# Moving the four loads of W_out to another DMA queue, and one sum of signs to a later place on VectorE

## The chip, the cores and the metric

The kernel runs on one core of a Trainium2 chip, in one launch. The metric is the time of the execution on the device in microseconds, as the median of repeated runs. Lower is better. A profile of one execution stands beside it; its span runs from the first to the last instruction of the core.

## The reference

Two layers read the same normalised input and are added to it: a linear attention with decay over chunks of 128 tokens, and a feed-forward network with ternary weights that keeps the 204 largest of 2048 hidden values of each token. Cut to what matters:

```python
# attention layer: B=4, T=1024, E=512, 16 heads of 32, chunks of 128
q, k, v = (x @ Wq), (x @ Wk), (x @ Wv)          # per head
q, k = _rotary(q), _rotary(k)
def step(kv, qkv):
    qi, ki, vi = qkv
    inter = jnp.einsum('bhcd,bhde->bhce', qi * q_decay[None, :, :, None], kv)
    scores = jnp.einsum('bhcd,bhsd->bhcs', qi, ki) * dmask[None]
    intra = jnp.einsum('bhcs,bhse->bhce', scores, vi)
    kv_new = r_C[None, :, None, None] * kv + jnp.einsum('bhcd,bhce->bhde', ki * k_decay[None, :, :, None], vi)
    return (kv_new, inter + intra)
attn = _rms_norm(attn, rms_w); return attn @ Wo
# feed-forward layer: N=2048
def ternary_quant(W):
    scale = jnp.mean(jnp.abs(W))
    q = jnp.clip(jnp.round(W / (scale + 1e-08)), -1.0, 1.0) * scale
    return W + jax.lax.stop_gradient(q - W)
z = x_flat @ ternary_quant(W_syn).T + b_syn
topv, _ = jax.lax.top_k(z, k)                    # k = 204 of 2048
hidden = jnp.where(z >= topv[:, -1:], jax.nn.relu(z), 0.0)
out = hidden @ ternary_quant(W_out).T + b_out
return layernorm(x + out, gamma, beta)
# both together
xn = _layernorm(x)
return x + attention(xn) + feed_forward(xn)
```

The mean of |W| over the whole matrix fixes the threshold of its ternary form, so no sign of W_out can be taken before all of W_out was read and summed.

## The kernel before

The 4096 tokens are 32 tiles of 128. A prologue prepares the weights, and then 31 steps run as a pipeline: in the step of tile t, TensorE makes the projections of tile t+1, the attention of tile t, the attention's output product of tile t-1 and the feed-forward's second product (`network_high`, `network_low`) of tile t-2. Each engine has its own program in its own `@block`, written out by hand; instructions of an engine run in that order, and semaphores (`wait_ge`, `then_inc`) hold them to one another. DMAs that SyncE issues go through its queue, those that ScalarE issues through another one. Before the change ScalarE issues the loads of Wq, Wk, Wv and of the four quarters of W_syn, and SyncE everything else, all transpositions by DMA among it.

W_out comes in four quarters of 1 MB, `out_in[0]` to `out_in[3]` (128 partitions with 8 KB each). Their places are used by others before. Quarters 2 and 3 lie where quarters 0 and 1 of W_syn were (the tile `woutT`), so they wait until these were made ternary (`syn_tern` 1, `syn_sign` 2). Quarter 0 lies in `hl`, where the ternary quarter 0 of W_syn is read by a DMA transposition (`synT0`) and, as its neighbour, by TensorE (`syn_flip`). Quarter 1 lies in a part of `area1` that nothing uses earlier. ScalarE then takes the sum of absolute values of each quarter (`sums("out", ...)`, L374) into a column of `pc`; its full-size output goes to `signs_b`, a scratch area (half of `pair_b`) that Wo's absolute sum (`wo_rows`, L398) and others also use, so that they run in one fixed order. TensorE sums the columns over the partitions (`sums_spread`, L877), and from the mean come the thresholds.

In the prologue VectorE makes the first guess of tile 0's threshold from the statistics of z (L1355, `guess_ready`). In the step of tile 0 ScalarE counts with that guess (`first_count`, L524), refines twice, and VectorE writes the masked copy of z (`below`, L1522), from which it takes maxima of 16 segments (`segments`, L1423). In between it makes the high and low halves of Wo (L1361, L1366).

The signs of W_out are taken by ScalarE (`sign("out", ...)`, L380), two for each quarter, and added by VectorE (`ternary_of_signs`, L1373 and L1377). SyncE transposes each quarter into `woutT` (`out_transpose`, L300). Quarter 1's ternary form lies in `hT`'s place, so the transposition of tile 0's hidden values (`high_transposed`, L308) waits for `outT1`, and TensorE's first `network_high` (L1043) waits for that and for all four quarters. `following_step` is VectorE's order in the step of tile 1.

## Time and profile before

| what | value |
|---|---|
| median of 3 runs | 987.05 us (986.56 to 988.97) |
| the profiled execution | 988.97 us, its span 987.2 us |
| TensorE (PE) busy | 931.5 us, 94% of the span |
| VectorE (DVE) busy | 861.2 us, 87% |
| GpSimd (POOL) busy | 757.8 us, 77% |
| ScalarE (ACT) busy | 591.2 us, 60% |
| mean granted clock of TensorE | 0.980 |

Busy time is an average over the whole; in the first 120 us, where the weights are prepared, the shares are lower and the engines wait for each other in turn. The timelines of the engines there, with the idle time in front of an instruction and what ended it, tell which wait comes last. The DMA share is that of 16 engines which all queues use together. The granted clock is 1.00 at 2.4 GHz and 0.50 at 1.2 GHz.

### The profile page before, as it was taken

What the parts mean: (1) busy time and instruction counts of PE and PEld (TensorE: products, weight loads), DVE (VectorE), ACT (ScalarE), POOL (GpSimd) and SP (SyncE); (2) the same over time, 40 slices, a digit from 0 to 9 for tenths busy, and PEclk for the clock granted to TensorE, in tenths of its full rate; (3) what the DMA queues carried; (4) which work ended last, traced back from release to release, by engine and by line L of the source; (5) the groups of instructions that cost most, each with busy time, mean ns of one, the idle gap of its engine ahead of it and who ended that gap; (6) DMA issues with size and microseconds to landing.
All of it is one profiled execution on the core that took longest, in us unless ns stands there. A gap on an engine that the chain in (4) does not pass through costs nothing.

```text
span 987.2 us, 19245 instructions
## 1 busy us (share of the span) xinstructions
PE 931.5 (94%) x6771; PEld 485.9 (49%) x6771; DVE 861.2 (87%) x2289; ACT 591.2 (60%) x782; POOL 757.8 (77%) x655
## 2 busy tenths in 40 slices
PE   5838799999999999999999999999999999999977
PEld 2414355554555555545555555455555554555533
DVE  6869688988889889889898898888988988989886
ACT  6778466665556666655566666555666665556551
POOL 1655768889888888898888888988888889888653
PEclk9977899999999999999999999999999999999999
DMA  9856645465555555565446546654466466444550
GB/s 326 266 174 115 118 78 115 89 119 118 97 93 83 115 103 101 119 117 92 92 86 118 113 92 118 117 98 89 85 118 110 94 118 115 98 92 83 97 97 32
DMA packets 322372, 111.08 MB, mean 113 GB/s; under 512 B 308449, under 2 KB 308705, under 8 KB 321505
## 3 DMA queue, kind: packets, MB, share of 16 engines
q1 hardware_dynamic: 318432, 102.42, 53.0%
q10 hardware_dynamic: 3840, 7.41, 2.1%
q8 instruction: 54, 0.88, 0.4%
q14 instruction: 46, 0.37, 0.1%
HBM read 24.34 MB, written 8.39 MB: 33 GB/s over the span
## 4 chain that ended last, share of the span: by engine, by line
PE 86%; DVE 5%; DMA 3%; issue 2%; ACT 1%; POOL 1%; SPq 1%; ACTq 0%; DVEq 0%; POOLq 0%
PE proj L933 44%; PE p_ffn L1043 11%; PE p_ffn L1051 10%; PE p_wo L1065 8%; PE p_av L1005 3%; PE sbank L996 3%; PE p_av L1016 3%; PE sbank L941 1%; DMA area<-hl 1%; DMA hl<-in_L_ffn_W_out_dram 1%; PE sbank L1108 1%; DMA area<-in_L_attn_Wq_dram 1%; SPq L269 0%; DMA woutT<-area 0%; SPq L264 0%
## 5 line engine op out<-in xcount | busy, mean ns | idle before, releaser
L933 PE MATMUL proj<-wqkv,xT 128*128 128x512 f16 x1152 | 261.5, 385 | 0.0
L933 PE MATMUL proj<-wsynT,xT 128*128 128x512 f16 x1024 | 238.9, 382 | 0.0
L933 PEld LDWEIGHTS proj<-wqkv,xT 128*128 128x128 f16 x1152 | 112.5, 99 | 127.8 <-issue 5.9
L933 PEld LDWEIGHTS proj<-wsynT,xT 128*128 128x128 f16 x1024 | 95.0, 98 | 100.9 <-issue 1.7
L743 POOL TENSOR_TENSOR hl<-area,hl 128x2048 f16<-128x2048 f32 x31 | 127.6, 4116 | 5.4 <-ACT hl L543 5.4
L1043 PE MATMUL p_ffn<-woutT,area 128*128 128x512 f16 x496 | 122.0, 391 | 7.9 <-DMA area<-hl 7.9
L1051 PE MATMUL p_ffn<-woutT,area 128*128 128x512 f16 x496 | 112.3, 379 | 0.0
L458 ACT ACTIVATE area<-area 128x1024 f16<-128x1024 f32 x64 | 64.1, 1049 | 77.4 <-POOL area L697 77.4
L1423 DVE MAX8 cand<-area 128x8 f32<-128x128 f32 x512 | 107.7, 277 | 1.1
L1311 DVE SCALAR_TENSOR_TENSOR area<-proj,c,gb 128x512 f32<-128x512 f32 x128 | 92.6, 744 | 5.3 <-PE proj L933 2.8
L748 POOL TENSOR_TENSOR ahl<-pair_a,ahl 128x512 f16<-128x512 f32 x32 | 37.1, 1159 | 78.0 <-DVE area L1522 75.2
L1522 DVE SCALAR_TENSOR_TENSOR area<-area,c 128x2048 f32<-128x2048 f32 x32 | 93.3, 2917 | 1.1
L1065 PE MATMUL p_wo<-wo,ahl 128*128 128x512 f16 x384 | 88.6, 380 | 2.4 <-POOL ahl L748 2.4
L548 ACT ACTIVATE pair_b<-pair_b,c 128x512 f32<-128x512 f32 x31 | 25.2, 812 | 103.4 <-DVE c L1517 103.4
L1475 DVE SCALAR_TENSOR_TENSOR area<-area,c 128x2048 f32<-128x2048 f32 x31 | 84.0, 2709 | 0.0
L517 ACT ACTIVATE diag<-ident,c 128x128 bf16<-128x128 f32 x32 | 12.9, 402 | 114.9 <-DVE c L1404 114.9
L1051 PEld LDWEIGHTS p_ffn<-woutT,area 128*128 128x128 f16 x496 | 48.5, 98 | 58.3
L1043 PEld LDWEIGHTS p_ffn<-woutT,area 128*128 128x128 f16 x496 | 47.2, 105 | 56.1 <-DMA area<-hl 8.3
L702 POOL TENSOR_TENSOR area<-area 128x512 f16<-128x512 f32 x64 | 74.7, 1190 | 0.0
L793 POOL TENSOR_TENSOR kvs<-state,rc 128x128 f32<-128x128 f32 x31 | 69.9, 2255 | 0.0
L543 ACT ACTIVATE hl<-area 128x2048 f16<-128x2048 f32 x31 | 59.2, 1909 | 16.5 <-DVE area L1475 16.5
L529 ACT ACTIVATE Pr<-area,c 128x2048 f16<-128x2048 f32 x32 | 63.8, 1993 | 0.9 <-DVE c L1482 0.9
(237 smaller groups left out, 1817.5 us busy)
## 6 DMA issues: line engine op xcount, KB each, us to landing
xrn<-in_L_attn_x_dram SPq DMA_DIRECT2D x32, 256.0 KB, 3.0
out_dram<-pair_b SPq DMA_DIRECT2D x32, 256.0 KB, 2.0
woutT<-in_L_ffn_W_syn_dram ACTq DMA_DIRECT2D x2, 1024.0 KB, 10.7
area<-in_L_ffn_W_syn_dram ACTq DMA_DIRECT2D x2, 1024.0 KB, 11.9
woutT<-in_L_ffn_W_out_dram SPq DMA_DIRECT2D x2, 1024.0 KB, 6.5
area<-in_L_attn_Wq_dram ACTq DMA_DIRECT2D x1, 1024.0 KB, 7.0
area<-in_L_attn_Wk_dram ACTq DMA_DIRECT2D x1, 1024.0 KB, 9.3
area<-in_L_attn_Wv_dram ACTq DMA_DIRECT2D x1, 1024.0 KB, 11.5
```

The costliest lines, as they stand in the source:

```text
L458: nc.scalar.activation(qks[:, m, :, 0:2 + m:1 + m, :], src.unsqueeze(2).to_broadcast([P, H, 2, DH]), ACT.Copy).then_inc(S["qk_hi"], 1)
L702: nc.gpsimd.tensor_tensor(qks[:, m, :, 2 - m, :], qk[:, b.par, m * E:(m + 1) * E].rearrange("p (h d) -> p h d", h=H), qks[:, m, :, 0, :], ...
L743: nc.gpsimd.tensor_tensor(hl[:, 1, :], src, hl[:, 0, :], ALU.subtract).then_inc(S["lo_ready"], 1)
L793: nc.gpsimd.tensor_tensor(kvs.rearrange("p (g e) -> p g e", g=HG), state.rearrange("p (g e) -> p g e", g=HG), k.unsqueeze(2).to_broadcast( ...
L933: last = nc.tensor.matmul(bank, xT[:, b.par, k, :], w, start=m == 0, stop=m == len(pairs) - 1)
L1043: nc.tensor.matmul(p_ffn, hT[:, k, :], woutT[:, k, :], start=k == 0, stop=False)
L1051: last = nc.tensor.matmul(p_ffn, hT[:, NB + k, :], woutT[:, k, :], start=False, stop=k == NB - 1)
L1065: last = nc.tensor.matmul(p_wo, ahl[:, l, g, :], wo[:, w, g, :], start=m == 0, stop=m == len(terms) - 1)
L1311: nc.vector.scalar_tensor_tensor(z[:, b.par, n * 512:(n + 1) * 512], proj[(b.par + 3 + n) % 2], gs, gb[:, n * 512:(n + 1) * 512], ALU.mult ...
L1423: nc.vector.max(cand[:, 0, 8 * n:8 * n + 8], masked[:, n * SEG:(n + 1) * SEG]).then_inc(S["seg_done"], 1)
L1475: nc.vector.scalar_tensor_tensor(dst, z[:, u.par, :], thr, z[:, u.par, :], ALU.is_ge, ALU.mult).then_inc(S["h_ready"], 1)
L1522: nc.vector.scalar_tensor_tensor(masked, z[:, t.par, :], t2, z[:, t.par, :], ALU.is_le, ALU.mult).then_inc(S["w_out"], 1)
```

## The change

The loads of W_out move from SyncE's queue to ScalarE's. Quarter 1 is issued in the prologue right after the last quarter of W_syn. Quarters 2 and 3 are issued after ScalarE's two signs of W_syn's quarter 1; ScalarE waits there for `syn_tern` 1. Quarter 0 is issued after tile 1's third projection was evicted, behind waits for `synT0` and `syn_flip` 4. The sum of quarter 1 is taken right behind that, ahead of the evictions of the flipped signs (`syn_flat`), and Wo's sum comes after it; the other three sums keep their place. On VectorE, in the step of tile 1, the sum of signs of quarter 1 moves from a place ahead of the second chunk of z (`z_chunk(b, 1)`) to one behind it, behind the addition of the attention, the last maxima and `so`, which itself moves ahead of the selection.

```diff
--- before.py
+++ after.py
@@ -237,9 +237,6 @@
             def load_x(n):
                 load(xr[:, n % RING, :], x[n * P:(n + 1) * P, :], f"x_loaded{n % 2}")
 
-            def load_out(q):
-                load(out_in[q], W_out.rearrange("(b p) n -> p b n", p=P)[:, q, :], f"out_loaded{q}")
-
             def load_tables():
                 load(gb, rows(b_syn, N), "rows_loaded")
                 for dst, src in ((qdec, t_qdec), (kdec, t_kdec), (rc, t_rc), (keep, t_keep), (iota, t_iota)):
@@ -280,18 +277,11 @@
                 load_wo()
                 load_x(2)
                 syn_transposed(0, 1)
-                load_out(2)
-                sp.wait_ge(S["syn_sign"], 2)
-                load_out(3)
                 load(boutx, rows(b_out, E), "bb_loaded")
                 load(bet, rows(beta, E), "bb_loaded")
                 load(gam, rows(gamma, E), "bb_loaded")
                 syn_transposed(2, 2)
                 qk_transposed(Tile(0, 0))
-                load_out(1)
-                sp.wait_ge(S["synT0"], 16)
-                sp.wait_ge(S["syn_flip"], 4)
-                load_out(0)
                 load(dmask, t_dmask, "dmask_loaded")
 
             def out_transpose(q):
@@ -367,8 +357,10 @@
                     act.wait_ge(S[f"{w}_loaded{q}"], 16)
 
                     n = 4 * (w == "out") + q
-                    if w == "out":
-                        act.wait_ge(*(S["wo_abs"], 1) if q == 2 else (S["out_abs"], (3, 1, 0).index(q) + 1))
+                    if w == "out" and q == 1:
+                        act.wait_ge(S["syn_flip"], 4)
+                    elif w == "out":
+                        act.wait_ge(*(S["wo_abs"], 1) if q == 2 else (S["out_abs"], 2 if q == 3 else 3))
                     else:
                         act.wait_ge(*(S["qkv_abs"], 3) if q == 0 else (S["syn_abs"], 1))
                     nc.scalar.activation(signs_b, (out_in if w == "out" else syn_in)[q], ACT.Abs,
@@ -394,7 +386,7 @@
             def wo_rows():
 
                 act.wait_ge(S["wo_scaled"], KB)
-                act.wait_ge(S["syn_flip"], 4)
+                act.wait_ge(S["out_abs"], 1)
                 nc.scalar.activation(signs_b, wo_in.rearrange("p b n -> p (b n)"), ACT.Abs,
                                      accum_out=pc[:, 57:58]).then_inc(S["wo_abs"], 1)
 
@@ -420,6 +412,9 @@
             def load_syn(q):
                 act.dma_start(syn_in[q].rearrange("p (b d) -> p b d", d=E),
                               W_syn.rearrange("(b p) d -> p b d", p=P)[:, 4 * q:4 * q + 4, :]).then_inc(S[f"syn_loaded{q}"], 16)
+
+            def load_out(q):
+                act.dma_start(out_in[q], W_out.rearrange("(b p) n -> p b n", p=P)[:, q, :]).then_inc(S[f"out_loaded{q}"], 16)
 
             def out_mean():
                 act.wait_ge(S["out_sum"], 1)
@@ -486,6 +481,7 @@
                 qkv_sums(1)
                 load_syn(2)
                 load_syn(3)
+                load_out(1)
                 qkv_sums(2)
                 normalised(second)
                 qkv_high(1)
@@ -500,15 +496,23 @@
 
                 sign("syn", syn_in[1], syn_other[1], syn_thr[1])
                 sign("syn", syn_in[1], syn_t[1], syn_thr[0])
+                act.wait_ge(S["syn_tern"], 1)
+                load_out(2)
+                act.wait_ge(S["syn_sign"], 2)
+                load_out(3)
                 qkv_out(second, 1)
                 qk_high(first)
                 sign("syn", syn_in[3], syn_other[3], syn_thr[1])
                 sign("syn", syn_in[3], syn_t[3], syn_thr[0])
                 qkv_out(second, 2)
+                act.wait_ge(S["synT0"], 16)
+                act.wait_ge(S["syn_flip"], 4)
+                load_out(0)
+                sums("out", (1,))
                 syn_flat(3)
                 heads_state(first)
                 wo_rows()
-                sums("out", (2, 3, 1, 0))
+                sums("out", (2, 3, 0))
 
             def diagonal(u):
 
@@ -1597,14 +1601,14 @@
                 z_chunk(b, 0)
                 probs(t, 2)
                 probs(t, 3)
-                ternary_of_signs(1, 9)
                 z_chunk(b, 1)
                 attention_added(u)
                 segments(t, 3)
-                selection(t)
                 dve.wait_ge(S["out_mean"], 1)
                 then(nc.vector.scalar_tensor_tensor(so, scale_out, 0.5 * XS / 16384.0, pc[:, 43:44], ALU.mult,
                                                     ALU.mult))
+                ternary_of_signs(1, 9)
+                selection(t)
                 z_chunk(b, 2)
 
             def step(dve, i, p):
```

The number of instructions of TensorE, VectorE and GpSimd, and their kinds, stay as they are; TensorE's and GpSimd's order too. Below, a row is a line of the kernel, the operation with output and inputs, and the semaphores that it waits for. First ScalarE in the prologue, around the signs of W_syn's quarter 1 (the sign into `hl`) before:

```order
L436 ACTIVATE area<-proj 128x512 [waits qkv_done]
L380 ACTIVATE pair_b<-woutT,pc 128x2048 [waits syn_thr]
L380 ACTIVATE hl<-woutT,pc 128x2048 [waits syn_thr]
L436 ACTIVATE area<-proj 128x512 [waits qkv_done]
L458 ACTIVATE area<-area 128x16x64 [waits rot_step]
```

and after:

```order
L431 ACTIVATE area<-proj 128x512 [waits qkv_done]
L372 ACTIVATE pair_b<-woutT,pc 128x2048 [waits syn_thr]
L372 ACTIVATE hl<-woutT,pc 128x2048 [waits syn_thr]
L417 DMA woutT<-in_L_ffn_W_out_dram 128x2048 [waits syn_tern]
L417 DMA woutT<-in_L_ffn_W_out_dram 128x2048 [waits syn_sign]
L431 ACTIVATE area<-proj 128x512 [waits qkv_done]
L453 ACTIVATE area<-area 128x16x64 [waits rot_step]
```

Two loads of W_out now stand between the signs and the next eviction of a projection, each with its wait. Further on ScalarE evicts, sums and counts. Before, from the eviction of tile 1's v to the last sum:

```order
L436 ACTIVATE v<-proj 128x512 [waits qkv_done]
L475 ACTIVATE wsynT<-sbank 128x512 [waits syn_flip] x2
L475 ACTIVATE wsynT<-p_av 128x512 [waits syn_flip]
L475 ACTIVATE wsynT<-p_ffn 128x512 [waits syn_flip]
L468 ACTIVATE stateD<-state 32x4x32 [waits constants]
L468 ACTIVATE stateD<-state 32x4x32 x3
L398 ACTIVATE pair_b,pc<-area 128x2048 [waits syn_flip,wo_scaled]
L374 ACTIVATE pair_b,pc<-woutT 128x2048 [waits wo_abs,out_loaded2]
L374 ACTIVATE pair_b,pc<-woutT 128x2048 [waits out_abs,out_loaded3]
L374 ACTIVATE pair_b,pc<-area 128x2048 [waits out_abs,out_loaded1]
L374 ACTIVATE pair_b,pc<-hl 128x2048 [waits out_abs,out_loaded0]
```

and after, from the same eviction on:

```order
L431 ACTIVATE v<-proj 128x512 [waits qkv_done]
L417 DMA hl<-in_L_ffn_W_out_dram 128x2048 [waits syn_flip,synT0]
L366 ACTIVATE pair_b,pc<-area 128x2048 [waits syn_flip,out_loaded1]
L470 ACTIVATE wsynT<-sbank 128x512 [waits syn_flip] x2
L470 ACTIVATE wsynT<-p_av 128x512 [waits syn_flip]
L470 ACTIVATE wsynT<-p_ffn 128x512 [waits syn_flip]
L463 ACTIVATE stateD<-state 32x4x32 [waits constants]
L463 ACTIVATE stateD<-state 32x4x32 x3
L390 ACTIVATE pair_b,pc<-area 128x2048 [waits out_abs,wo_scaled]
L366 ACTIVATE pair_b,pc<-woutT 128x2048 [waits wo_abs,out_loaded2]
L366 ACTIVATE pair_b,pc<-woutT 128x2048 [waits out_abs,out_loaded3]
L366 ACTIVATE pair_b,pc<-hl 128x2048 [waits out_abs,out_loaded0]
```

The load into `hl` and the sum of quarter 1 (`area`, `out_loaded1`) have come in front of the evictions into `wsynT`. On SyncE's queue nothing takes the place of the four loads: the bias rows follow the transposition of W_syn's quarter 0, and the load of `dmask` follows the two of tile 0's q and k.

On VectorE, in the step of tile 1, the weighting of the scores (L1388), the sum of signs (into `area`), the chunk of z, the attention's addition and the maxima stood like this:

```order
L1388 SCALAR_TENSOR_TENSOR pair_a<-sbank,c,dmask 128x512 [waits ss_done,al_ready,scores_done] x2
L1373 TENSOR_TENSOR area<-area,pair_b 128x2048 [waits out_sign]
L1311 SCALAR_TENSOR_TENSOR area<-proj,c,gb 128x512 [waits z_done]
L1397 SCALAR_TENSOR_TENSOR xrn<-p_wo,c,xrn 128x512 [waits factor_step,beta_added,wo_done]
L1423 MAX cand<-area 128x8 [waits top_step,w_out]
L1423 MAX cand<-area 128x8 x3
L1528 TENSOR_SCALAR c<-c 128x1 [waits sum3]
```

and now:

```order
L1392 SCALAR_TENSOR_TENSOR pair_a<-sbank,c,dmask 128x512 [waits ss_done,al_ready,scores_done] x2
L1315 SCALAR_TENSOR_TENSOR area<-proj,c,gb 128x512 [waits z_done]
L1401 SCALAR_TENSOR_TENSOR xrn<-p_wo,c,xrn 128x512 [waits factor_step,beta_added,wo_done]
L1427 MAX cand<-area 128x8 [waits top_step,w_out]
L1427 MAX cand<-area 128x8 x3
L1608 SCALAR_TENSOR_TENSOR c<-c,pc 128x1 [waits out_mean]
L1377 TENSOR_TENSOR area<-area,pair_b 128x2048 [waits out_sign,seed]
L1532 TENSOR_SCALAR c<-c 128x1 [waits sum3]
```

The sum of signs has gone behind the four others.

## Rows read from the trace of the kernel before

**Rows 1.** The page, part 4: the chain that ended last, by engine

```profile
PE 86%; DVE 5%; DMA 3%; issue 2%; ACT 1%; POOL 1%; SPq 1%; ACTq 0%; DVEq 0%; POOLq 0%
```

**Rows 2.** Waits of TensorE (PE), 135 to 980 us: total, times, longest

```profile
PE p_ffn L1043 <- DMA area<-hl: 2.8, 1, 2.8
```

**Rows 3.** Timeline of TensorE: start, us, engine, line, op, [idle before <-releaser]

```profile
50.42 0.27 PE L860 MATMUL p_ffn<-ident,pc 128*1 128x128 f32 x1 [0.54 <-ACT pair_b L398]
...
74.81 0.61 PE L996 MATMUL sbank<-area 96*128 96x128 f16 x4 [9.57 <-DVE Pr L1388]
...
105.88 1.89 PE L933 MATMUL proj<-wsynT,xT 128*128 128x512 f16 x8
...
117.89 3.60 PE L1043 MATMUL p_ffn<-woutT,area 128*128 128x512 f16 x8 [5.14 <-DMA area<-hl]
```

**Rows 4.** Timeline of ScalarE (ACT) from 25 to 65 us

```profile
34.96 0.57 ACT L436 ACTIVATE area<-proj 128x512 f32<-128x512 f32 x1
...
41.31 0.60 ACT L436 ACTIVATE v<-proj 128x512 f32<-128x512 f32 x1
44.67 1.20 ACT L475 ACTIVATE wsynT<-sbank 128x512 f16<-128x512 f32 x2 [2.77 <-PE sbank L888]
...
62.60 1.91 ACT L374 ACTIVATE pair_b<-hl 128x2048 f16<-128x2048 f32 x1 [1.64 <-DMA hl<-in_L_ffn_W_out_dram]
...
64.51 1.99 ACT L524 ACTIVATE Pr<-area,c 128x2048 f16<-128x2048 f32 x1
```

**Rows 5.** Timeline of VectorE (DVE) from 58 to 71 us

```profile
58.00 0.43 DVE L1355 SCALAR_TENSOR_TENSOR c<-pc 128x1 f32<-128x1 f32 x1
...
66.94 2.34 DVE L1366 SCALAR_TENSOR_TENSOR wo<-area,pc,wo 128x2048 f16<-128x2048 f32 x1
...
70.01 2.35 DVE L1522 SCALAR_TENSOR_TENSOR area<-area,c 128x2048 f32<-128x2048 f32 x1
```

**Rows 6.** Timeline of GpSimd (POOL) at 59 us

```profile
59.52 1.65 POOL L663 TENSOR_TENSOR c<-c 128x1 f32<-128x1 f32 x1 [0.74 <-DVE c L1301]
```

**Rows 7.** Timeline of SyncE's queue (SPq) from 35 to 40 us

```profile
35.42 1.95 SPq L269 DMA_TRANSPOSE wsynT<-hl  x1
37.42 1.57 SPq L235 DMA_DIRECT2D woutT<-in_L_ffn_W_out_dram  x2
```

**Rows 8.** DMA issues, 37 to 40 us: last number is us to landing

```profile
wsynT<-hl SPq DMA_TRANSPOSE x1, 4.4
```

**Rows 9.** Windows: stretch, us, busy us of each engine, PEclk, DMA share, GB/s

```profile
15.00:20.00 5.00, 4.63 (x14) 1.71 (x12) 3.16 (x15) 4.01 (x6) 1.18 (x1) 1.00 1.05 386
20.00:25.00 5.00, 5.00 (x25) 2.62 (x24) 4.90 (x6) 5.00 (x5) 0.45 (x1) 1.00 0.74 275
80.00:85.00 5.00, 4.71 (x66) 2.73 (x58) 4.76 (x20) 4.42 (x6) 3.86 (x5) 0.92 0.81 149
120.00:125.00 5.00, 5.00 (x22) 1.99 (x21) 2.24 (x10) 1.11 (x2) 1.92 (x3) 0.83 1.14 207
```

**Rows 10.** DMA queues, 6 to 7 us: packets, MB, share; q10 is ScalarE's

```profile
q10 hardware_dynamic: 174, 0.35, 93.6%
q1 hardware_dynamic: 132, 0.02, 12.9%
```

**Rows 11.** Timeline of VectorE from 108 to 115 us

```profile
108.44 0.74 DVE L1311 SCALAR_TENSOR_TENSOR area<-proj,c,gb 128x512 f32<-128x512 f32 x1
...
109.76 0.85 DVE L1423 MAX8 cand<-area 128x8 f32<-128x128 f32 x4
...
114.14 0.83 DVE L1606 SCALAR_TENSOR_TENSOR c<-c,pc 128x1 f32<-128x1 f32 x1
```

**Rows 12.** The chain in order of time: start us, us, what

```profile
106.84 1.69 DVE area L1373
108.54 4.84 DMA woutT<-area
113.45 4.40 DMA area<-hl
```

## Prediction, made before the changed kernel was run

> **What bounds the kernel now.** I read the page first: TensorE makes up 86% of the chain that ended last, over a span of 987.2 us [rows 1]. From 135 us on TensorE waits almost nowhere, 2.8 us at its worst place [rows 2]. So the body runs at TensorE's pace, and nothing in it is touched. What the change can move is the moment at which TensorE enters that body: its row at 117.89 us, the first product with W_out's transpose, after 5.14 us idle for a DMA [rows 3]. A microsecond there is a microsecond of the whole, since later waits are too few to absorb it.
>
> Then I read the timelines of the start. The engines are late twice. First, ScalarE finishes the last absolute sum of W_out only at 64.4 us, because that quarter lands at 62.6, and its next instruction, the first count of tile 0, starts at 64.51 [rows 4]. VectorE had the guess that this count wants at 58.43 (58.00 and 0.43) [rows 5]. TensorE's 9.57 us idle before 74.81 is the same delay passed on through VectorE [rows 3]. Second, before 117.89 the chain is VectorE's sum of signs of quarter 1 (106.75 to 108.44), its transposition issued at 108.54, and the transposition of tile 0's hidden values, which waits for that one [rows 11, 12].
>
> **Part one: the loads of W_out move to ScalarE's queue.** Quarter 1 is issued 40 us earlier, behind W_syn. At 386 GB/s a quarter takes 2.7 us [rows 9], so it lands long before 42 us. The issue costs ScalarE at most 0.8 us of its queue (two in 1.57 us on SyncE's) [rows 7], beside work with about as much slack: nothing.
>
> Quarters 2 and 3 now make ScalarE wait for `syn_tern` 1, which comes when SyncE's transposition goes, at 35.42 [rows 7]. ScalarE was ready at 34.96 [rows 4], so 0.46 us of wait and two issues of 0.4 to 0.8 us: 1.2 to 2.0, I take 1.4 us. Behind them stand one eviction of a projection, the cast of tile 0's q and k, the signs of W_syn's quarter 3 and another eviction. That last one starts at 41.31 now and would start at 42.7 and end at 43.3. ScalarE is idle for 2.77 us after it, before 44.67 [rows 4]; this idle time covers the 1.4 us, as long as it isn't used twice.
>
> It is used twice, by quarter 0. ScalarE now waits for `synT0` before it may issue that load, and the sum of quarter 1 comes next, 1.91 and 0.1 us as the sum at 62.60 [rows 4]. The transposition behind `synT0` lands 4.4 us after its issue at 35.42, at 39.8 [rows 8]. But that was with quarters 2 and 3 behind it in its own queue; now they run beside it. No row shows a load beside a transposition. From below: an even split of the engines' time adds as much as the transposition itself needs, some 2.7 us, so 42.5, and ScalarE doesn't wait. From above: both loads are served first, 5.4 us, so 45.2. The nearest row is between 6 and 7 us, where both queues have work: 174 packets of one against 132 of the other, though the first moved 0.35 MB and the second 0.02 [rows 10]. Turns go by packet there, not by bytes, and W_out's rows are 8 KB where the transposition's packets are small, so I take 45.2. ScalarE then issues at 45.2, sums to 47.7, and its evictions of the flipped signs start at 47.7 instead of 44.67, 3.0 us later. So does the absolute sum of Wo (L398), for which TensorE's row at 50.42 waits [rows 3]. Behind that row stand the third and fourth chunk of tile 0's z, and with them the guess: 58.43 becomes 61.4. With the even split it is 43.3 plus 0.5 for the issue plus 2.0, 45.8 instead of 44.67: 1.1 us, and the guess at 59.6.
>
> The three remaining sums, 2.1 us apart each, follow the Wo sum and end about 59.6, before that guess. So the count starts with the guess. From there the path to VectorE's masked copy (70.01) takes: GpSimd's power op, which ends 2.74 us after the guess (59.52 and 1.65) [rows 6]; 0.2 us for the row shift; the low half of Wo, 2.3 (66.94 now); and 0.8 to the copy, as now from 69.2 to 70.01 [rows 5]. That is 6.1 us instead of 11.6. The gain is 5.5 us less what the guess loses: **5.5 − 3.0 = 2.5 us**, or 5.5 − 1.1 = 4.4 with the even split. Down to 106 us I find VectorE, ScalarE and GpSimd handing each other work without a fixed date in between, so all of it moves along. The masks that were loaded behind quarter 0 leave earlier: no cost.
>
> **Part two: VectorE's sum of signs of quarter 1 goes behind four other things.** Now it runs when `probs` ends, at 106.75. In its new place the third chunk of z comes first; it waits for TensorE's product at 105.88, which takes 1.89 us [rows 3], so it starts at 107.8. It and attention's addition take 1.3 us (108.44 to 109.76 now), the four maxima 0.8, and `so` between nothing and the 0.83 that it has at 114.14; I take 0.2 to 0.3, as its neighbours on one column mostly overlap [rows 11]. The sum starts at about 110.1 and, at the 1.69 us it takes now, ends at 111.8 instead of 108.44. The bounds are 3.1 and 4.0 by `so` alone. **The cost is 3.4 us**: the transposition that leaves at 108.54 leaves that much later, and nothing else was last there. What moves ahead gains nothing, since TensorE had its third chunk in time. Selection is later by the same sum, and its flag is wanted only in the middle of the product at 117.89 [rows 3].
>
> **The clock.** TensorE's idle time before 117.89 grows from 5.1 to some 8.5 us. After the 5.1 us the granted clock stays at the 1.2 GHz level until about 121.7 (a mean of 0.83 from 120 to 125), 3.8 us; after the 9.57 us before 74.81, until about 80.8 (0.92 from 80 to 85), 5.6 us from the restart at about 75.2 [rows 3, 9]. Half of 1.8 us is at most 0.9; by the length of the gap I take 0.3.
>
> **The sum**: −2.5 + 3.4 + 0.3 = +1.2 us, for a span of 988.4. The profiled execution took 988.97 us, 1.8 more than its span, and the median is 987.05; against the median, which is what will be compared, that is **988.2 us**. A measurement of this kernel tells 0.3%, 3.0 us, from no change.
>
> **Rivals.** (1) *Even split*: −4.4 + 3.4 + 0.3 = −0.7, 986.3 us. For it: the packets of a transposition might be grouped. Against: the counts [rows 10].
>
> (2) *Loads and transpositions slow each other down*. Place: DMA engines from 36 us on, where W_syn's two transpositions, quarters 2, 3 and 0 and the bias rows come to some 15 us of work in two queues. If the mixture runs a fifth slower, `synT0` and W_syn's second transposition land 2 to 3 us later, TensorE and ScalarE wait for them, and the gain of 2.5 is gone: +3.4 + 0.3, and up to 1 more. Time 991. It decides against the kernel from a loss of 1.8 us there (990.0). For it: quarter 0 will stand in front of W_syn's second transposition. Against: where both queues have loads, they move 0.37 MB in a microsecond together, close to one queue's 386 GB/s [rows 9, 10].
>
> (3) *No byte lands sooner*. Then ScalarE still waits for W_out as now, the first gain is 0, and the time is 987.05 + 3.7 = 990.8. Against it: from 20 to 25 us the DMA engines are busy for only 0.74 of the time [rows 9], which is room for quarter 1, and quarter 0 no longer stands behind it.
>
> The Trainium skill speaks against the change here: "DMA: Bandwidth & Descriptors", in its rules for kernel authors, says that spreading DMAs over several issuing engines gives no bandwidth and saves only issue time. Taken alone it gives rival 3; no row here contradicts it on bandwidth, and what the change has besides is the earlier date of issue.
>
> (4) *The second part is free*: some other wait is last before 117.89. Then −2.5 or −4.4 stands alone, some 983.5 us. Against it: the chain has the two transpositions back to back, 108.54 and 4.84 us, then 113.45 and 4.40 [rows 12].
>
> **Chances.** Forecast 0.50, rival 1 0.25, rival 2 0.13, rival 3 0.04, rival 4 0.08. The range: below, the even split with 3.1 and no clock loss, 985.7, and a little for the spread of the runs; above, 4.0 and 0.9 on the forecast give 989.5, and it reaches into rival 2: 985.3 to 990.7. Faster by over 0.3% (under 984.1) is most of rival 4 alone: 0.07. Slower (over 990.0) is rivals 2 and 3, less the milder half of each's range: 0.15. Within: 0.78.
>
> **What would show it.** `synT0`'s landing at 45.2 against 42.5; ScalarE's sum of quarter 1 around 46; the first count at 61.5 (59.7 with rival 1); the masked copy at 67.5; the transposition of quarter 1 issued at about 109.4; TensorE's first W_out product at 118.8, or 117 and less with rival 1. TensorE entering before 115 or after 121 would make the prediction wrong, and so would any new wait of TensorE behind 135 us.

## The result, and the profile after

The changed kernel takes 992.7 us (median of 6 runs, 990.6 to 996.4) against 987.2 us for the kernel before beside it (6 runs, 985.9 to 989.0): a ratio of 1.0058, 95% interval 1.0035 to 1.0082. Measured again on another occasion (the run e3_after_again below) the ratio was 1.0042, 1.0027 to 1.0056. The change makes the kernel 4 to 5.5 us slower. The prediction said 988.2 us, 1.2 us slower and within what can be told from no change; it was wrong, and 992.7 lies above its range. (One execution of the kernel before, out of 84, took 1401.9 us; medians are hardly touched by it.)

The profiled execution of the changed kernel took 989.12 us, with a span of 987.1, so the two profiled executions are equally long. The one of before, 988.97 us, stands high among its runs, and the one of after lies below all six timed runs of its kernel. Where they part again is told at the end of this section. First the chain that ended last by engine, from the page, for [rows 1]:

```profile
PE 85%; DMA 4%; DVE 4%; POOL 3%; issue 3%; SPq 0%; ACT 0%; ACTq 0%; DVEq 0%; POOLq 0%
```

and TensorE's wait from 135 to 980 us, for [rows 2]:

```profile
PE p_ffn L1047 <- DMA area<-hl: 1.6, 1, 1.6
```

The body still runs at TensorE's pace. TensorE's timeline, for [rows 3], with two more rows of the same stretch (start us, us, engine, line, operation, idle time ahead and its releaser):

```profile
46.96 3.61 PE L937 MATMUL proj<-wsynT,xT 128*128 128x512 f16 x16 [2.98 <-DMA wsynT<-hl]
54.56 0.27 PE L864 MATMUL p_ffn<-ident,pc 128*1 128x128 f32 x1 [3.98 <-ACT pair_b L390]
54.92 3.18 PE L937 MATMUL proj<-wsynT,xT 128*128 128x512 f16 x8
...
74.98 0.61 PE L1000 MATMUL sbank<-area 96*128 96x128 f16 x4 [11.03 <-DVE Pr L1392]
...
120.70 3.32 PE L1047 MATMUL p_ffn<-woutT,area 128*128 128x512 f16 x8 [7.87 <-DMA area<-hl]
```

TensorE enters the body at 120.70 instead of 117.89 us, 2.81 later. It is idle for 2.98 us for the first transposition of W_syn, which it did not wait for before, and for 3.98 us where it waited 0.54 us. ScalarE, for [rows 4]:

```profile
46.85 0.33 ACTq L417 DMA_DIRECT2D hl<-in_L_ffn_W_out_dram  x1
47.28 1.91 ACT L366 ACTIVATE pair_b<-area 128x2048 f16<-128x2048 f32 x1 [5.29 <-DMA wsynT<-hl]
...
49.19 1.06 ACT L470 ACTIVATE wsynT<-sbank 128x512 f16<-128x512 f32 x2
...
52.41 1.91 ACT L390 ACTIVATE pair_b<-area 128x2048 f16<-128x2048 f32 x1
...
58.69 1.91 ACT L366 ACTIVATE pair_b<-hl 128x2048 f16<-128x2048 f32 x1
...
64.23 2.00 ACT L528 ACTIVATE Pr<-area,c 128x2048 f16<-128x2048 f32 x1 [3.54 <-DVE c L1359]
```

The last sum of W_out starts at 58.69 us instead of 62.60, 3.9 us sooner, as the change wants it. But the first count starts at 64.23, only 0.28 us sooner than before, because it now waits 3.54 us for VectorE's guess. VectorE, for [rows 5] and [rows 11]:

```profile
63.77 0.43 DVE L1359 SCALAR_TENSOR_TENSOR c<-pc 128x1 f32<-128x1 f32 x1
...
70.17 2.35 DVE L1526 SCALAR_TENSOR_TENSOR area<-area,c 128x2048 f32<-128x2048 f32 x1
...
109.22 0.86 DVE L1427 MAX8 cand<-area 128x8 f32<-128x128 f32 x4
110.00 0.14 DVE L1608 SCALAR_TENSOR_TENSOR c<-c,pc 128x1 f32<-128x1 f32 x1
110.17 1.73 DVE L1377 TENSOR_TENSOR area<-area,pair_b 128x2048 f16<-128x2048 f16 x1
```

The guess has moved from 58.00 to 63.77, by 5.8 us, and the masked copy from 70.01 to 70.17: the whole gain of the earlier loads is gone at that point. The sum of signs then starts at 110.17 instead of 106.75. The chain in order of time, for [rows 12]:

```profile
110.17 1.74 DVE area L1377
111.91 0.02 issue
111.93 4.25 DMA woutT<-area
...
116.24 4.41 DMA area<-hl
```

SyncE's queue and the landings, for [rows 7] and [rows 8] (the number at the end of the second piece is us from issue to landing):

```profile
34.33 5.80 SPq L266 DMA_TRANSPOSE wsynT<-hl  x1
```

```profile
wsynT<-hl SPq DMA_TRANSPOSE x1, 12.5
```

The same transposition that landed 4.4 us after its issue now takes 12.5 us, and its issue holds SyncE for 5.80 us instead of 1.95. What the queues moved shows why. For [rows 10], first the microsecond from 38 to 39 before the change, when the transposition was alone:

```profile
q1 hardware_dynamic: 836, 0.21, 116.7%
```

then the one from 40 to 41 in the changed kernel, where ScalarE's queue (q10) has quarters 2 and 3:

```profile
q10 hardware_dynamic: 40, 0.33, 78.0%
q1 hardware_dynamic: 46, 0.01, 5.2%
```

Forty packets of 8 KB and 46 of 256 bytes: in this microsecond the queues take turns packet by packet, so the transposition gets 46 packets through in the time in which it had 836. From 36 to 38 us it gets none through at all.

**The end of the two profiled executions.** TensorE reaches the scores of the last tile at 951.45 us, against 948.98 before, so 2.5 of the 2.8 us are still there. The last step gives them back. TensorE's first `network_high` of the last step, before the change:

```profile
958.84 3.59 PE L1043 MATMUL p_ffn<-woutT,area 128*128 128x512 f16 x8 [2.77 <-DMA area<-hl]
```

and after it:

```profile
960.59 1.90 PE L1047 MATMUL p_ffn<-woutT,area 128*128 128x512 f16 x8 [1.59 <-DMA area<-hl]
```

Eight products take 3.59 us in one execution, at the 1.2 GHz level, and 1.90 us in the other, at 2.4 GHz. The changed kernel is 1.75 us late at the start of this row and level at its end. That differs from one execution to the next (in a second profiled one of the changed kernel the same row took 2.72 us), and is why the medians, and not this pair, carry the comparison.

### The profile page after: what moved, and what is told of

The parts are those of the page before. It is cut to its first block, busy times and chain, and to the rows that moved or that the text cites. A ratio compares the mean times of both kernels' runs of the same rounds, so it can differ in the third digit from the quotient of the medians.

```text
span 987.1 us, 19245 instructions
## 1 busy us (share of the span) xinstructions
PE 929.5 (94%) x6771; PEld 484.8 (49%) x6771; DVE 858.9 (87%) x2289; ACT 590.8 (60%) x782; POOL 758.8 (77%) x655
## 4 chain that ended last, share of the span: by engine, by line
PE 85%; DMA 4%; DVE 4%; POOL 3%; issue 3%; SPq 0%; ACT 0%; ACTq 0%; DVEq 0%; POOLq 0%
PE proj L937 44%; PE p_ffn L1047 11%; PE p_ffn L1055 10%; PE p_wo L1069 8%; PE p_av L1009 3%; PE p_av L1020 3%; PE sbank L1000 3%; PE sbank L945 1%; DMA area<-in_L_ffn_W_syn_dram 1%; DMA area<-in_L_attn_Wk_dram 1%; PE sbank L1112 1%; DVE cand L1427 1%; DMA area<-in_L_attn_Wo_dram 1%; DMA area<-area 0%; DMA area<-hl 0%
## 5 line engine op out<-in xcount | busy, mean ns | idle before, releaser
L1047 PE MATMUL p_ffn<-woutT,area 128*128 128x512 f16 x496 | 118.8, 383 | 9.5 <-DMA area<-hl 9.5
L1055 PE MATMUL p_ffn<-woutT,area 128*128 128x512 f16 x496 | 112.3, 379 | 0.1
L706 POOL TENSOR_TENSOR area<-area 128x512 f16<-128x512 f32 x64 | 72.7, 1157 | 0.0
```

The costliest lines, as they stand in the source:

```text
L706: nc.gpsimd.tensor_tensor(qks[:, m, :, 2 - m, :], qk[:, b.par, m * E:(m + 1) * E].rearrange("p (h d) -> p h d", h=H), qks[:, m, :, 0, :], ...
L1047: nc.tensor.matmul(p_ffn, hT[:, k, :], woutT[:, k, :], start=k == 0, stop=False)
L1055: last = nc.tensor.matmul(p_ffn, hT[:, NB + k, :], woutT[:, k, :], start=False, stop=k == NB - 1)
```

## The experiments

Two theories stand against each other for the 4 to 5.5 us. A: the order on VectorE costs 3.4 us as predicted, and the loads fail to bring their 2.5 us, because they collide with the transpositions of W_syn (rival 2 of the prediction). B: the loads bring what was predicted and the order on VectorE, or the two together, costs more. All kernels of one batch ran beside the kernel before: 987.16 us in the first (e1 to e5), 987.45 in the second (e6 to e9), 987.62 in the third (e10 to e13).

| kernel | first product with W_out's transpose, us | median us (lowest to highest, runs) | ratio to before |
|---|---|---|---|
| before | 117.89 | 987.16; 987.45; 987.62 | 1 |
| e1 loads only | 117.71 | 988.42 (985.5 to 995.4, 12) | 1.0019 [1.0000, 1.0038] |
| e2 order on VectorE only | 120.58 | 990.43 (988.9 to 991.5, 8) | 1.0030 [1.0018, 1.0042] |
| e3 the change again | 121.00 | 991.20 (988.3 to 996.0, 12) | 1.0042 [1.0027, 1.0056] |
| e5 quarter 1 only | 114.33 | 983.23 (982.8 to 984.4, 5) | 0.9960 [0.9946, 0.9973] |
| e6 = e5, quarter 0 earlier | 113.40 | 983.26 (981.7 to 984.5, 5) | 0.9956 [0.9943, 0.9969] |
| e7 quarters 1, 0 on ScalarE | 116.21 | 986.88 (985.6 to 988.1, 11) | 0.9995 [0.9986, 1.0004] |
| e8 quarters 1, 2, 3 on ScalarE | 114.64 | 985.66 (982.2 to 992.5, 12) | 0.9987 [0.9969, 1.0006] |
| e9 = e6, bias rows later | 117.42 | 986.77 (984.7 to 987.2, 11) | 0.9987 [0.9979, 0.9996] |
| e10 = e5 + order on VectorE | 117.70 | 987.96 (986.2 to 988.8, 10) | 1.0004 [0.9994, 1.0013] |
| e11 = e5, quarters 2, 3 after `synT0` | 118.39 | 988.10 (986.2 to 989.4, 12) | 1.0001 [0.9991, 1.0012] |

The second column is from each kernel's one profiled execution. Median less first product is 868.9 to 871.0 us in every row, while the first product moves by 7.6 us: the moment at which TensorE enters the body sets most of the time, as the prediction had it. It sets the time to 2 or 3 us and not better: taken from one and the same execution, the time less the first product still runs from 868.4 to 871.1 us over all fourteen traces.

**The loads alone.** The change, with VectorE's order of before:

```diff
                 probs(t, 3)
+                ternary_of_signs(1, 9)
                 z_chunk(b, 1)
...
+                selection(t)
...
-                ternary_of_signs(1, 9)
-                selection(t)
```

> The changed kernel with VectorE's order of before (the sum of signs of quarter 1 again ahead of the second chunk of z); the loads stay on ScalarE's queue. Theory M (the new loads beside the transpositions delay W_syn's transposition, and with it ScalarE and TensorE, by an amount that varies from execution to execution): the first count does not start earlier than the 64.5 us of before, in some executions later; time 988 to 991 us and a spread of several us. Theory V (only VectorE's later sum costs time, the loads bring what was forecast): 2.5 us faster than before, 984.7 us.

988.42 us: 1.3 us slower than before in the median (interval 0 to 0.38%), where the prediction's own term was 2.5 us faster. Its trace has the late transposition again (it lands 11.0 us after its issue) and TensorE's wait for Wo's sum. TensorE's wait for the transposition itself is not there: TensorE was late in this execution by another wait (3.36 us for VectorE), and then found the transposition landed:

```profile
54.27 0.37 PE L864 MATMUL p_ffn<-ident,pc 128*1 128x128 f32 x1 [3.34 <-ACT pair_b L390]
...
117.71 0.61 PE L1047 MATMUL p_ffn<-woutT,area 128*128 128x512 f16 x1 [5.05 <-DMA area<-hl]
```

The first product comes at 117.71 us, 0.18 sooner than before, instead of 2.5. The remaining 1.5 us of the median are not in this trace; the runs of e1 spread over 9.9 us, and one trace can't stand for them. Either way the loads bring nothing, and theory B falls on its first half.

**The order on VectorE alone.** The second hunk of the change on the kernel before:

```diff
                 probs(t, 3)
-                ternary_of_signs(1, 9)
                 z_chunk(b, 1)
...
-                selection(t)
...
+                ternary_of_signs(1, 9)
+                selection(t)
```

> The kernel before with only VectorE's new order in the step of tile 1; all loads as before. By the sum of the prediction the transposition of quarter 1 leaves 3.4 us later and all behind it: +3.4 us, 990.6 us, with the small spread of before. If VectorE's sum was not last there (rival 4 of the prediction): no difference, 987.2 us. If V alone explains the result: +5.5 us.

990.43 us, 3.3 us slower (1.8 to 4.1 by the interval). TensorE's wait grew from 5.14 to 7.83 us:

```profile
120.58 1.89 PE L1043 MATMUL p_ffn<-woutT,area 128*128 128x512 f16 x4 [7.83 <-DMA area<-hl]
```

The term of 3.4 us was right for the row that it was worked out for: quarter 1's transposition is issued at 111.84 instead of 108.54 us, 3.3 later. TensorE's first product is only 2.7 us later in this trace. About 0.5 us comes back because that transposition is followed by the next after 4.3 us instead of 4.9; it is the same in the other two kernels traced with the new order, the change (4.3) and e10 (4.3), against 4.8 in e1 and 4.9 in e5 with the old one.

**The change again.** The changed kernel as it is, beside the two.

> The changed kernel once more, unaltered, for a second trace and more times. Theory M: W_syn's first transposition, issued at 34.3 us, lands at another time than the 46.8 us of the first trace, by a microsecond or more, and the median stays near 992 us with a spread of several us. Theory V: the same landing, the same spread as before's 3 us.

991.20 us, 4.0 slower than before; 1.3 and 3.3 make 4.6. The two parts add up within what was measured, and no extra cost of the two together is needed.

**Quarter 1 alone.** The kernel before, with only the early load of quarter 1:

```diff
                 load_syn(3)
+                load_out(1)
...
                 qk_transposed(Tile(0, 0))
-                load_out(1)
                 sp.wait_ge(S["synT0"], 16)
```

> The kernel before with one edit: quarter 1 of W_out is loaded on ScalarE's queue right behind W_syn; quarters 2, 3 and 0 stay on SyncE's, and both engines' other order stays. No load runs beside a transposition in another queue. Theory M: quarter 0 lands some 2.5 to 4 us earlier (by 59 to 60 us instead of 62.6), the first count starts at 60.5 to 61.5 instead of 64.5, and the kernel is 2.5 to 4 us faster: 983 to 984.5 us, with a small spread. If the early load itself harms (bandwidth, Wo's landing), it is not faster.

983.23 us, 3.9 us faster, and the runs lie within 1.6 us. The last sum and the count behind it:

```profile
58.45 1.91 ACT L373 ACTIVATE pair_b<-hl 128x2048 f16<-128x2048 f32 x1 [4.85 <-DMA hl<-in_L_ffn_W_out_dram]
...
60.65 2.00 ACT L527 ACTIVATE Pr<-area,c 128x2048 f16<-128x2048 f32 x1 [0.20 <-DVE c L1358]
```

The count starts at 60.65 instead of 64.51. It now waits 0.20 us for the guess, which has itself become 2.2 us later than before (60.18 against 58.00), since TensorE waited 2.80 us for W_syn's second transposition; so both are last together. Quarter 0 is issued at 53.35 us, nearly as before (53.96), but the megabyte of quarter 1 no longer stands ahead of it, and it lands after 5.1 us and not 8.6. `synT0` lands after 4.4 us, as before. This is the part of the change that is worth having, and in the change it is hidden under the others.

**Which of the other loads costs it.** Two kernels from e1: in the first, quarters 2 and 3 went back to SyncE's queue, in the second, quarter 0.

```diff
-                act.wait_ge(S["syn_tern"], 1)
-                load_out(2)
-                act.wait_ge(S["syn_sign"], 2)
-                load_out(3)
...
                 syn_transposed(0, 1)
+                sp_load_out(2)
+                sp.wait_ge(S["syn_sign"], 2)
+                sp_load_out(3)
```

> The loads-only kernel (e1_loads_only) with quarters 2 and 3 back on SyncE's queue behind W_syn's first transposition; quarters 1 and 0 stay on ScalarE's. No load runs beside the first transposition, one (quarter 0) beside W_syn's second. Theory M, with the harm in quarters 2 and 3: the first transposition lands by 40 us as before, ScalarE issues quarter 0 at about 42, the absolute sum of Wo runs at its old time, and of the 3.9 us that e5_quarter1_only gained at least 2.5 are back: 983 to 985 us with a small spread. If quarter 0 in its own queue does the harm: near e1_loads_only, 987 to 989 us, with the wide spread.

```diff
                 qk_transposed(Tile(0, 0))
+                sp.wait_ge(S["synT0"], 16)
+                sp.wait_ge(S["syn_flip"], 4)
+                sp_load_out(0)
...
-                act.wait_ge(S["synT0"], 16)
-                act.wait_ge(S["syn_flip"], 4)
-                load_out(0)
```

> The loads-only kernel (e1_loads_only) with quarter 0 back on SyncE's queue behind the transpositions; ScalarE no longer waits for W_syn's first transposition, while quarters 2 and 3 stay beside it on ScalarE's queue. Theory M, harm in the mixture: the first transposition still lands at 46 to 47 us and TensorE still waits for it, but ScalarE's sums run early; the last sum is then late again by its load (61 to 62 us): 985.5 to 987.5 us. If only ScalarE's wait for that transposition costs time and not the mixture: as e5_quarter1_only, 983.2 us.

e7 takes 986.88 us, slower than its 983 to 985. `synT0` is on time there, but quarter 0 is issued at 39.75 us on ScalarE's queue, ahead of W_syn's second transposition, and TensorE waits for that one and then runs at the 1.2 GHz level:

```profile
53.40 3.23 PE L939 MATMUL proj<-wsynT,xT 128*128 128x512 f16 x8 [2.50 <-DMA wsynT<-xrn]
```

e8 takes 985.66 us, and `synT0` is late:

```profile
46.72 3.61 PE L940 MATMUL proj<-wsynT,xT 128*128 128x512 f16 x16 [1.89 <-DMA wsynT<-hl]
...
59.44 1.91 ACT L372 ACTIVATE pair_b<-hl 128x2048 f16<-128x2048 f32 x1 [6.46 <-DMA hl<-in_L_ffn_W_out_dram]
```

With quarter 1 early in all four, the medians are 983.2 (e5: the others on SyncE), 985.7 (2 and 3 on ScalarE), 986.9 (0 on ScalarE) and 988.4 (all). Quarters 2 and 3 beside the first transposition cost 1.5 to 2.4 us, quarter 0 ahead of the second one 2.8 to 3.7. The intervals say how firm that is: those of e5 and e7 lie well apart, so the cost of quarter 0 is shown; those of e5 and e8, and of e7 and e1, overlap, so the cost of quarters 2 and 3 by themselves is not clear of the spread. (In e7 and e8, as in the change, the sum of quarter 1 also stands ahead of the flipped signs, which e5 leaves as it was; that is part of their difference to e5.)

The traces say more about where the harm is done. In e8 it lands 12.4 us after its issue, TensorE waits 1.89 us for it, and yet the first product is at 114.64 us, only 0.3 after e5's. There ScalarE does not wait for it, and TensorE reaches the row behind Wo's sum at 50.16 us without waiting. With quarter 0 on ScalarE's queue as well (e1), that row comes at 54.27 and the first product at 117.71. So in the traced executions the late landing by itself costs little. Quarter 0 adds two things at once, ScalarE's wait for that landing ahead of its sums, and a second transposition that lands at 54.2 us instead of 50.8; no run parts the two.

**Where a transposition ends up when a load runs beside it.** Landing of `synT0`'s transposition after its issue, from the DMA issues of each profiled execution: 4.4 to 4.6 us in before, e2, e5, e6, e7, e9, e10 and e11, where no load of W_out is in another queue meanwhile; 11.0 (e1), 12.4 (e8), 12.5, 11.8, 14.1 and 14.6 us (the change, four executions), where quarters 2 and 3 come beside it. No value lies between. The spread of the runs goes with it: 7.7 to 10.3 us in e1, e3 and e8, 1.6 to 3.2 us in the other seven. Two more profiled executions of the changed kernel asked whether the landing is what varies:

> The changed kernel, one more profiled execution. If the landing of synT0 is what varies from one execution to the next, it lands at another time than 46.3 or 46.8 us, and the whole execution is later or earlier by about as much. If it lands at 46 to 47 again while the time differs by over 1.5 us from 989.1, the variation is somewhere else.

> The changed kernel, one more profiled execution, as the run before it: the landing of synT0 and the time of the execution should move together if that landing makes the spread.

The one took 989.35 us, the other 992.50. ScalarE's sum of quarter 1, which starts 0.5 us after `synT0`'s landing, in the first

```profile
48.93 1.91 ACT L366 ACTIVATE pair_b<-area 128x2048 f16<-128x2048 f32 x1 [6.84 <-DMA wsynT<-hl]
```

and in the second:

```profile
50.11 1.91 ACT L366 ACTIVATE pair_b<-area 128x2048 f16<-128x2048 f32 x1 [7.28 <-DMA wsynT<-hl]
```

against 47.28 and 46.73 in the two before. The landing does vary, by 3.4 us over four executions, and the latest goes with the longest time (first product at 122.02). But the order is not strict: 46.73 went with 991.09 us and 48.93 with 989.35. The four traces side by side, in us (after is the first profile):

| changed kernel | sum of quarter 1 | TensorE's row behind Wo's sum | guess | first product | time |
|---|---|---|---|---|---|
| e3 | 46.73 | 54.01 | 64.03 | 121.00 | 991.09 |
| after | 47.28 | 54.56 | 63.77 | 120.70 | 989.12 |
| e12 | 48.93 | 56.20 | 64.05 | 120.97 | 989.35 |
| e13 | 50.11 | 57.38 | 64.97 | 122.02 | 992.50 |

TensorE's row follows the landing, at a distance of 7.3 us, and the first product follows the guess, at 56.9 to 57.1. Between the row and the guess lie 10.0, 9.2, 7.9 and 7.6 us, less the later the landing (in e3, 0.76 of it is a wait for W_syn's second transposition). In the first two TensorE comes back at that row at the 1.2 GHz level (eight products in 3.43 and 3.18 us); in the last two it had paid for the low level before it, in time in which it would have waited for ScalarE anyway (sixteen products in 5.30 and 6.45 us instead of 3.61), and the eight took 1.89. So 3.4 us of landing become 1.2 us of guess. The landing makes part of the spread; executions of 995 us were not caught in a trace, and what they look like stays open.

**The same queue, without a load beside the transposition.** From e5: quarters 2 and 3 on ScalarE's queue, but only once `synT0` has landed, with W_syn's second transposition behind them.

```diff
                 qkv_out(second, 2)
+                act.wait_ge(S["synT0"], 16)
+                act.wait_ge(S["syn_tern"], 1)
+                load_out(2)
+                act.wait_ge(S["syn_sign"], 2)
+                load_out(3)
                 syn_flat(3)
...
-                load_out(2)
-                sp.wait_ge(S["syn_sign"], 2)
-                load_out(3)
...
+                sp.wait_ge(S["out_loaded3"], 16)
                 syn_transposed(2, 2)
```

> The kernel with only quarter 1 issued early, and quarters 2 and 3 issued on ScalarE's queue as in the change, but only once synT0 has landed; W_syn's second transposition waits until they have landed. So the queue is the change's, and no load runs beside a transposition. Theory (a load beside a transposition is what makes both late and the times spread): synT0 lands at about 39.8 as before the change, the loads take 5.5 us, W_syn's second transposition ends some 0.6 us later than before, 983.5 to 984.5 us, and the spread of the runs is 3 us or less. Rival (ScalarE's queue as such, or its issue work, is to blame): 985.7 us or more and a spread of 8 to 10 us, as in the kernel with quarters 2 and 3 beside synT0.

Half of this came true. `synT0` lands after 4.4 us, and the twelve runs lie within 3.2 us: it is the load beside the transposition that makes it late, not ScalarE's queue, and the spread went away with it. The time was missed, 988.1 instead of 983.5 to 984.5. The landings and SyncE's queue show why:

```profile
woutT<-in_L_ffn_W_out_dram ACTq DMA_DIRECT2D x2, 1024.0 KB, 8.7
boutx<-in_L_ffn_b_out_dram SPq DMA_DIRECT2D x1, 256.0 KB, 4.7
...
wsynT<-hl SPq DMA_TRANSPOSE x1, 4.4
```

```profile
50.43 1.95 SPq L269 DMA_TRANSPOSE wsynT<-xrn  x1
```

The three bias rows now come first and take the DMA engines from 39 to 45 us, beside the loads, which land after 8.7 us and not 5.5. The second transposition leaves at 50.43 instead of about 43, so VectorE waits 5.52 us for the third chunk of z. The transpositions of q and k and the load of quarter 0 stand behind it in SyncE's queue and are late too. That load is what the first count waits for in the end, since the guess is done at 64.21 us:

```profile
63.02 1.91 ACT L371 ACTIVATE pair_b<-hl 128x2048 f16<-128x2048 f32 x1 [5.44 <-DMA hl<-in_L_ffn_W_out_dram]
64.93 1.99 ACT L530 ACTIVATE Pr<-area,c 128x2048 f16<-128x2048 f32 x1
```

I had carried the loads' time over from a place where they ran alone.

**Better than both kernels.** From e5, quarter 0 goes ahead of the transpositions of tile 0's q and k (e6), and from that the bias rows go behind W_syn's second transposition (e9):

```diff
                 syn_transposed(2, 2)
-                qk_transposed(Tile(0, 0))
                 sp.wait_ge(S["synT0"], 16)
                 sp.wait_ge(S["syn_flip"], 4)
                 load_out(0)
+                qk_transposed(Tile(0, 0))
```

> The kernel of e5_quarter1_only with quarter 0 issued ahead of the transpositions of tile 0's q and k instead of behind them, in the same queue of SyncE's. In e5_quarter1_only the last sum ended at 60.4 us and the guess was there at 60.6, so both were last together; its guess was late by W_syn's second transposition, for which TensorE waited 2.8 us. Expected: the sum no longer counts and the guess sets the start; at most 0.5 us faster than e5_quarter1_only, 982.7 to 983.5 us. If TensorE's scores, now 2.7 us later, are last: slower than that, 984 to 986 us.

> The kernel of e6_quarter0_ahead with the three loads of bias rows moved behind W_syn's second transposition in SyncE's queue. That transposition should land at about 47.5 us instead of 50.1, TensorE's wait of 2.8 us for it and the low clock behind it should go, and the guess should come some 4 us earlier, at 56 to 57 us. If nothing else is last: 980 to 981.5 us. If TensorE's sum over the partitions, which stands behind the scores in its order, holds ScalarE's second count: 982 to 983.5 us. No load runs beside a transposition in another queue, so a small spread.

e6 takes 983.26 us, the same as e5. Quarter 0 is no longer waited for, but the scores are:

```profile
59.44 0.83 PE L999 MATMUL sbank<-area 96*128 96x128 f16 x12 [3.21 <-DMA area<-area]
```

e9 takes 986.77 us, a miss: the bias rows, which GpSimd adds up in the middle of its order, now come so late that the guess waits for GpSimd:

```profile
60.87 0.15 DVE L1355 TENSOR_SCALAR c<-pc 128x1 f32<-128x1 f32 x1 [6.56 <-POOL pc L735]
```

Either of e5 and e6 beats the kernel before by 0.4% and the changed kernel by 0.8 to 0.9%.

**The order on VectorE on the better base.** e5 with the second hunk of the change.

> The kernel with only quarter 1 issued early (983.2 us), plus the new order on VectorE. Theory: the sum of signs costs the same 3.3 us as it did alone on the kernel before, since the chain before TensorE's first product with W_out's transpose is the same there: 983.2 + 3.3 = 986.5 us, the first product at about 117.5 and some 7.8 us of idle time before it. Rival: with a faster start the selection or the out_mean wait is no longer hidden and the two edits do not add: then 988 or more, or, if the sum of signs has slack there, under 985.

987.96 us, where the theory had 986.5 and the rival 988 or more. The first product comes 3.4 us later than in e5, at 117.70 us, after 7.81 us of idle time, as the theory says. By the medians the difference is 4.7 us, or 0.44% by the ratios, 1.4 us more than the entry explains; the two profiled executions don't start alike either (the first transposition is issued at 34.36 us in e5 and at 35.84 in e10), so I leave that 1.4 us unexplained; whether the two edits add exactly stays open.

## Why the prediction was wrong

**The bound was read right.** The time follows TensorE's entry at its first product with W_out's transpose: in eleven kernels the entry runs from 113.40 to 121.00 us, and the median follows within 2.1 us. The first measurement of the changed kernel lies outside that: of its 5.5 us the entry has 2.8 in the first trace and at most 4.1 over four, and the rest stays open.

**Part two was right.** The sum of signs starts at 110.17 us (110.1 predicted), `so` takes 0.17 us of VectorE, and the term of 3.4 us measured 3.3 us alone (1.8 to 4.1), 2.7 us of it at the entry. Rival 4, that it is free, is refuted by the same run.

**Part one failed, in the step on quarter 0 and `synT0`.** The prediction put the gain at 5.5 − 3.0 = 2.5 us; e1 measured a loss of 1.3 us. The 5.5 us, the path without waiting for quarter 0, was right: from the guess's end at 64.20 to the masked copy is 5.97 us (6.1 predicted), and the sums end 3.5 us ahead of the guess. The 3.0 us that the guess would lose was 5.8 us: 5.5 − 5.8 leaves no gain, and the masked copy is in fact 0.2 us later than before. (That is 2.8 of the 3.8 us between the forecast and e1's median; most of the rest is the part of e1's median that its trace does not show.) The 5.8 us have two pieces, TensorE's later return from its wait (4.1) and the clock (1.6):

- The landing. The prediction took "both loads are served first, 5.4 us, so 45.2" as the upper bound. `synT0` landed at some 46.8 us in the first profile (46.3 to 49.6 over four). That the loads come first was read rightly from [rows 10]. The 5.4 us were two loads alone on the engines; here they take 8.1 us to land, and the transposition is not done when they are. The DMA queues of the changed kernel, microsecond by microsecond; the last column is SyncE's share × 16 engines / its packets (shares over 100% come from packets whose times overlap):

| us | ScalarE's queue: packets, share | SyncE's queue: packets, share | ns for one of SyncE's |
|---|---|---|---|
| 38 to 39 | 54, 113.7% | 206, 23.2% | 18 |
| 40 to 41 | 40, 78.0% | 46, 5.2% | 18 |
| 42 to 43 | 16, 16.1% | 423, 89.8% | 34 |
| 43 to 44 | 8, 9.9% | 162, 127.4% | 126 |
| 44 to 45 | 3, 5.8% | 55, 137.8% | 401 |
| 45 to 46 | 1, 0.1% | 782, 106.3% | 22 |

  Alone, before the change, one took 1.167 × 16 / 836, 22 ns. So the small packets cost no more than that while the loads are served; they only wait for their turn. The slow ones come from 42 to 45 us, when ScalarE's queue has nearly run dry, and cost some 2.7 us more than at 22 ns. That stretch is what the bound lacked. Why those packets are slow no run here shows. Wo's sum comes 4.1 us later (52.41 against 48.27), and the row of TensorE that waits for it as well (54.56 against 50.42).
- A second wait ends at the same place, and the sum had put it at nothing. W_syn's second transposition lands 11.5 us after its issue instead of 6.9, at 54.8 instead of 50.3 us, and the eight products at 54.92 need it. So with Wo's sum on time, and this landing where it is, TensorE would still have made them over 4 us late. In e7, where Wo's sum is on time (TensorE's row at 50.64), it is this wait and the clock behind it that make the guess late, 62.25 instead of 58.00. The prediction had it only in rival 2.
- The clock, which the prediction asked about only at 117.89 us. TensorE was idle for 2.98 us, ran sixteen products at full rate (3.61 us), was idle for 3.98 us, and then the eight products at 54.92 took 3.18 us; the same eight took 1.89 us at 50.54 before. The granted clock from 55 to 58 us was 0.56, so the 1.2 GHz level for most of it. From the row at 54.56 to the guess are 9.21 us, against 7.58 before: 1.6 us more, 1.3 of them in these eight products. 4.1 and 1.6 make the 5.8 us. That split is the first trace's; the table of the four traces above shows how it shifts.

**Rival 2 was the right mechanism**, with the place it named, though the landings came later than its 2 to 3 us: both transpositions of W_syn late, `synT0` 7 us later than before and 1.6 us (up to 4.4) behind the forecast's own landing, and quarter 0 ahead of the second one costing 2.8 to 3.7 us (e5 to e7, e8 to e1). It gave 991 us; 991.2 and 992.7 were measured. The argument that held its chance at 0.13 was the weak place: that two queues together move 0.37 MB in a microsecond was read where both had loads, and carried over to a mixture of loads and small packets. Rival 1, the even split of the engines' time, is refuted by shares of 78.0% and 5.2% in the same microsecond. Rival 3, that no byte lands sooner, is refuted: W_out's last sum comes 3.9 us sooner, and e5 gains 3.9 us. The Trainium skill's rule behind it ("DMA: Bandwidth & Descriptors", rules for kernel authors: several issuing engines give no bandwidth) agrees with the traces as far as it goes: 0.34 MB in the microsecond from 40 to 41 us over two queues, 0.37 MB over one before. It speaks of the bytes; what decided here is that the transposition's small packets had to wait for the loads'.

**The clock before 117.89** was put at 0.3 us for a longer idle time. The traces show no such term: after 7.9 us of idle time the eight products took 3.32 us in the changed kernel, 3.60 us after 5.14 before. The first sixteen products take 5.0 to 6.5 us in the six traces with 7.8 to 7.9 us of idle time, and 5.2 to 6.5 in the eight with 4.9 to 5.2.

## What to carry to other kernels

A load in another DMA queue is not free for a transposition in the first: where turns go by packet, as here, a transposition of 256-byte packets stands nearly still while 8 KB packets are served, and it lands later by the whole length of the loads and more (7 us here). How much of that reaches the time depends on what stands behind it: in e8's trace, where ScalarE does not wait for it, very little does. Move a load to where the DMA engines have room and no transposition is under way, and leave the rest in the transposition's own queue behind it: one quarter of W_out, moved that way, was worth 3.9 us, and moving the other three as well turned that into a loss. When a wait is added to an engine in a prologue, price the clock too: after 3.98 us of idle time TensorE came back at half its rate, just where the chain was waiting for it, though after 2.98 us a little earlier it had come back at the full one. And look at every wait that ends near the one that is moved: here two ended within half a microsecond of each other, and the sum had only one of them.

## What the runs showed of the hardware

- The issue of W_syn's first transposition held SyncE for 1.90 to 2.83 us in the kernels without a load of W_out in the other queue, and for 5.47 to 7.16 us in the executions with two loads in the other queue.
- A packet of a transposition took 22 ns in the mean alone (38 to 39 us, before) and 18 ns beside 8 KB packets (40 to 41 us, after). In the changed kernel packets of 126 and 401 ns in the mean came from 43 to 45 us, when the other queue had 8 and 3 packets in a microsecond.
- Executions of one kernel spread over 1.6 to 3.2 us (e2, e5 to e7, e9 to e11) or 7.7 to 10.3 us (e1, e3, e8), and the wider ones are those with a load beside the first transposition; the kernel before spread over 4.0 to 4.8 us, but in 23 to 29 runs, and e5 and e6 have only five runs each. A change can cost reproducibility without its best runs getting slower: the best run of e8 was 982.18 us, as good as e5's 982.82.
